# A decoder layer on one core: the context blocks loaded a pair ahead into other rooms, and the last quarter of w_out loaded earlier

## What is computed

```python
# x: (4, 1024, 1024)   ctx_1024: (4, 1024, 512)
qkv = layernorm(x) @ w_qkv                      # 16 heads of 64, causal softmax attention
x = x + attention(qkv) @ w_out
query = ctx_1024 @ Wq.T + bq                    # (4, 1024, 128)
key   = ctx_1024 @ Wk.T + bk
attn  = softmax(query @ key.T)                  # 1024 x 1024
x = x + layernorm(x) @ attn.T
x = x + gated_experts(layernorm(x))             # 8 experts, rank 8, argmax gate
```

## Time and profile before

| what | value |
|---|---|
| median of 3 runs | 2772.9 us (2771.0 to 2775.31) |
| the profiled execution | 2772.5 us, of which the span is 2770.6 us |
| TensorE matmul busy | 2404.3 us (87%) |
| VectorE busy | 1884.6 us (68%) |
| ScalarE busy | 782.0 us (28%) |
| GpSimd busy | 717.5 us (26%) |
| mean granted TensorE clock | 0.954 of full |
| DMA, mean | 146 GB/s |
| chain that ended last, TensorE's share | 59% |

### The profile page before, as it was taken

One profiled execution on the slowest core, in us unless ns is written; L12 is line 12 of the kernel. 1 busy time (PEld: TensorE's weight loads), 2 busy tenths in 40 slices (PEclk: granted clock), 3 DMA queues, 4 the chain that ended last, 5 costly groups with the idle time before them and its releaser, 6 DMA issues.

```text
span 2770.6 us, 37859 instructions
## 1 busy us (share of the span) xinstructions
PE 2404.3 (87%) x14389; PEld 1186.3 (43%) x14389; DVE 1884.6 (68%) x3421; ACT 782.0 (28%) x1557; POOL 717.5 (26%) x981
## 2 busy tenths in 40 slices
PE   0588888689898999869998999969989999986997
PEld 0233444344454444444444444434444444434544
DVE  4577887646876767755786777764696777764566
ACT  1033333321213333322212333431221333332110
POOL 3122433213402222212421222221330222221220
PEclk9899999899999999979999999989999999998997
DMA  6678787856746776775753777774773677776543
GB/s 177 216 174 182 161 214 179 189 140 145 146 108 126 141 151 135 140 181 129 147 125 100 150 139 143 146 186 109 158 147 106 117 149 146 143 154 159 107 76 91
DMA packets 986009, 403.97 MB, mean 146 GB/s; under 512 B 937116, under 2 KB 946332, under 8 KB 985828
## 3 DMA queue, kind: packets, MB, share of 16 engines
q1 hardware_dynamic: 985828, 401.56, 65.8%
HBM read 133.05 MB, written 33.55 MB: 60 GB/s over the span
## 4 chain that ended last, share of the span: by engine, by line
PE 59%; DVE 19%; DMA 10%; issue 6%; ACT 3%; POOL 2%; SPq 1%; ACTq 0%; POOLq 0%; DVEq 0%
PE ps_p L537 8%; PE ps_p L538 8%; PE ps_p L539 8%; DMA r<-pn 8%; PE ps_s L537 6%; PE ps_s L538 6%; PE ps_s L539 6%; PE ps_s L582 6%; PE ps_o L607 5%; DVE pn L816 4%; DVE peak L853 3%; ACT probs L742 2%; DVE bn L821 2%; DMA qk<-in_x 2%; PE ps_s L587 1%
## 5 line engine op out<-in xcount | busy, mean ns | idle before, releaser
L1080 POOL TENSOR_SCALAR pn<-probs,rden 128x640 f16<-128x640 f32 (+7 forms) x512 | 391.9, 778 | 1332.7 <-DVE rden L865 827.1
L742 ACT ACTIVATE probs<-ps_s,low,back 128x640 f32<-128x640 f32 (+7 forms) x512 | 421.7, 827 | 950.8 <-DVE low L856 840.1
L816 DVE SCALAR_TENSOR_TENSOR pn<-probs,rden,pn 128x640 f16<-128x640 f32 (+7 forms) x512 | 476.3, 962 | 193.1 <-POOL pn L1080 192.8
L537 PE MATMUL ps_p<-r,w 128*128 128x512 f16 x1344 | 515.1, 383 | 3.1 <-DVE qk L816 3.1
L538 PE MATMUL ps_p<-r,w 128*128 128x512 f16 x1344 | 514.2, 383 | 0.0
L539 PE MATMUL ps_p<-r,w 128*128 128x512 f16 x1344 | 513.7, 382 | 0.0
L582 PE MATMUL ps_s<-qk 64*128 64x512 f16 (+3 forms) x2304 | 239.0, 332 | 107.9 <-ACT probs L742 97.9
L853 DVE TENSOR_REDUCE peak<-ps_s 128x2 f32<-128x1280 f32 (+3 forms) x128 | 241.4, 1886 | 92.8 <-PE ps_s L587 90.3
L607 PE MATMUL ps_o<-r,vn 128*64 128x512 f16 (+3 forms) x2304 | 210.9, 339 | 39.3 <-issue 30.0
L539 PEld LDWEIGHTS ps_p<-r,w 128*128 128x128 f16 x1344 | 132.5, 99 | 162.1 <-issue 6.3
L582 PEld LDWEIGHTS ps_s<-qk 64*128 64x128 f16 x2304 | 90.0, 95 | 252.3 <-ACT probs L742 147.4
(11 more groups left out here) (167 smaller groups left out, 3554.0 us busy)
## 6 DMA issues: line engine op xcount, KB each, us to landing
w<-w_pairs SPq DMA_DIRECT2D x72, 512.0 KB, 4.0
qk<-in_x SPq DMA_DIRECT2D x32, 512.0 KB, 4.3
r<-wo_pairs SPq DMA_DIRECT2D x16, 1024.0 KB, 7.3
w_raw<-in_x SPq DMA_DIRECT2D x32, 512.0 KB, 4.6
out<-r SPq DMA_DIRECT2D x32, 512.0 KB, 2.9
r<-in_w_qkv SPq DMA_DIRECT2D x24, 512.0 KB, 5.8
w_raw<-in_w_qkv SPq DMA_DIRECT2D x24, 512.0 KB, 5.1
w_pairs<-w SPq DMA_DIRECT2D x24, 512.0 KB, 5.5
```

The costliest lines, as they stand in the source:

```text
L537: pe.matmul(ps, lh, rh, start=start and k == ks[0], stop=False)
L742: act.activation(probs_part(q, j, w), ps_s[:, j, scores(q)], ACT.Exp, bias=low[:, n % 2, i:i + 1], scale=sc, accum_out=den[:, n % 2, i:i + ...
L816: dve.scalar_tensor_tensor(out=to, in0=bank, scalar=scale, in1=rounded, op0=ALU.mult, op1=ALU.subtract).then_inc(ok, 1)
L1080: pool.tensor_scalar(to, src, scale, 1.0, ALU.mult, ALU.mult).then_inc(ok, 1)
```

## The change

Three things change, in every tail.

`ctx_raw` becomes the two rooms of `w_raw`. JI0 and JI1 stand behind T6 of the pair before, ahead of KI; they wait for the last raw weight (batch 0) or the last output of the batch before. JI2 and JI3 wait until JL0 and JL1 are through. RI0 and RI1, which use the same rooms, now wait for JL2 and JL3, and stand behind T5 and T6. Each room has its own semaphore.

OI3 stands behind T2, where it waits for nothing that is open.

The steps JH, JL, G, QH and QL stand earlier in the strings of ScalarE, VectorE and TensorE: G0 where it was, G1 ahead of M0, G2 ahead of B00, G3 behind S7, and B10 straight behind B01.

```diff
 PE_TAIL = """
-    S2 S3 M1- S4 G0 S5 M0 S6 G1 B00 S7 B01 G2 B10 G3 B11 M1 B20 N0 B21 N1 B30 N2 ...
+    S2 S3 M1- S4 G0 S5 G1 M0 S6 G2 B00 S7 G3 B01 B10 B11 M1 B20 N0 B21 N1 B30 N2 ...
 DVE_TAIL = """
-    X0 L70- L71- CL21 R0 X1 L00 L01 X2 R1 L10 L11 R2 X3 KL L20 L21 OL1- R3 JL0 X4 L30 L31 R4 X5 QL0 JL1 L40 L41
-    R5 OL0 X6 L50 L51 QL1 JL2 R6 X7 L60 L61 R7 RA0 L70 L71 QL2 JL3 RA1 QL3 LB0 OL1 CX0 LL0 LB1 CR0 RA2 CX1 CLO0
+    X0 L70- L71- CL21 R0 X1 L00 L01 X2 R1 L10 L11 R2 X3 KL JL0 R3 OL1- X4 L20 L21 QL0 JL1 R4 L30 L31 X5 L40
+    L41 QL1 JL2 R5 OL0 X6 L50 L51 R6 QL2 JL3 X7 L60 L61 R7 QL3 RA0 L70 L71 RA1 LB0 OL1 CX0 LL0 LB1 CR0 RA2 CX1 CLO0
 ACT_TAIL = """
-    E00 E01 CH21 E10 E11 E20 E21 KH E30 E31 JH0 OH1- E40 E41 QH0 JH1 E50 E51 OH0 E60 E61 QH1 JH2 E70 E71 QH2 JH3
+    E00 E01 CH21 E10 E11 E20 E21 KH JH0 E30 E31 OH1- QH0 JH1 E40 E41 E50 E51 QH1 JH2 OH0 E60 E61 QH2 JH3 E70 E71
 SP_TAIL = """
-    OI0 JI0 OI1 T0 T1 OI2 T2 JI1 T3 T4 JI2 RI0 RI1 OI3 T5 JI3 T6 T7 WD0+ WD1+ WD2+ RI2 RI3 ...
+    OI0 OI1 T0 T1 OI2 T2 OI3 JI2 T3 T4 JI3 T5 RI0 T6 RI1 T7 WD0+ WD1+ WD2+ RI2 RI3 ...
 for pair in range(PAIRS - 2, BATCH * PAIRS, PAIRS):
-    ONCE["SP", pair, "T6"] = "KI"
+    ONCE["SP", pair, "T6"] = "JI0 JI1 KI"
-        ctx_raw = vt16[:, :, :].rearrange("p s d -> p (s d)").bitcast(F32).rearrange("p (c d) -> p c d", c=CC)
+        ctx_raw = w_raw[:, :, :].rearrange("p s (c d) -> p s c d", c=CC)
                     elif kind == "JI":
-                        if i > 0:
-                            sp.wait_ge(j_ok, 4 * b + i)
-                        else:
-                            sp.wait_ge(v_in, 16 * PAIRS * (b + 1))
-                        sp.dma_start(ctx_raw[:, :, :], ctx_t[b, :, :, i * CQ:(i + 1) * CQ]).then_inc(j_in, 16)
+                        if i >= 2:
+                            sp.wait_ge(j_ok, 4 * b + i - 1)
+                        elif b == 0:
+                            sp.wait_ge(w_ok, 3 * PAIRS)
+                        else:
+                            sp.wait_ge(y_ok, TB * b)
+                        sp.dma_start(ctx_raw[:, i % 2, :, :], ctx_t[b, :, :, i * CQ:(i + 1) * CQ]).then_inc(j_in[i % 2], 16)
                     elif kind == "RI":
                         if i >= 2:
                             sp.wait_ge(x1_ok, T - 1)
-                        elif b == 0:
-                            sp.wait_ge(w_ok, 3 * PAIRS)
-                        else:
-                            sp.wait_ge(y_ok, TB * b)
+                        else:
+                            sp.wait_ge(j_ok, 4 * b + 3 + i)
```

More of the change, by code:

```diff
@@ L58 @@
 PE_TAIL = """
-    S2 S3 M1- S4 G0 S5 M0 S6 G1 B00 S7 B01 G2 B10 G3 B11 M1 B20 N0 B21 N1 B30 N2 B31 N3 B40 N4 B41 N5 B50 N6 B51 N7
+    S2 S3 M1- S4 G0 S5 G1 M0 S6 G2 B00 S7 G3 B01 B10 B11 M1 B20 N0 B21 N1 B30 N2 B31 N3 B40 N4 B41 N5 B50 N6 B51 N7
     B60 B61 B70 B71 Z00 Z01 Z10 Z11 Z20 Z21 F0 Z30 Z31 F1 D0 Z40 Z41 F2 D1 U0 Z50 Z51 F3 D2 U1 Z60 Z61 F4 D3 U2
@@ L86 @@
 SP_TAIL = """
-    OI0 JI0 OI1 T0 T1 OI2 T2 JI1 T3 T4 JI2 RI0 RI1 OI3 T5 JI3 T6 T7 WD0+ WD1+ WD2+ RI2 RI3 CT0 LT0 CT1 RI4
+    OI0 OI1 T0 T1 OI2 T2 OI3 JI2 T3 T4 JI3 T5 RI0 T6 RI1 T7 WD0+ WD1+ WD2+ RI2 RI3 CT0 LT0 CT1 RI4
     LT1 RI5 CT2 CT3 RI6 CT4 CT5 RI7 CT6 CT7 AI0+ AI1+ AI2+ AT0+ AT1+ AI3+ LT2 AT2+
@@ L280, in decoder_layer @@
         d_bn, d_mv, d_ve, d_rs, d_sh, d_xn, d_hi, d_lo, t3_in = sems("d_bn d_mv d_ve d_rs d_sh d_xn d_hi d_lo t3_in")
-        k_in, kh_ok, kl_ok, j_in, jh_ok, j_ok, g_mm, qh_ok, ql_ok = sems(
-            "k_in kh_ok kl_ok j_in jh_ok j_ok g_mm qh_ok ql_ok")
+        k_in, kh_ok, kl_ok, jh_ok, j_ok, g_mm, qh_ok, ql_ok = sems(
+            "k_in kh_ok kl_ok jh_ok j_ok g_mm qh_ok ql_ok")
+        j_in = [sem(f"j_in{s}") for s in range(2)]
         n_mm, n_peak, n_low, ce_ok, n_den, n_r, n_hi, n_lo = sems("n_mm n_peak n_low ce_ok n_den n_r n_hi n_lo")
@@ L491, in rest @@
                     elif kind == "JI":
-                        if i > 0:
-                            sp.wait_ge(j_ok, 4 * b + i)
-                        else:
-                            sp.wait_ge(v_in, 16 * PAIRS * (b + 1))
-                        sp.dma_start(ctx_raw[:, :, :], ctx_t[b, :, :, i * CQ:(i + 1) * CQ]).then_inc(j_in, 16)
-                    elif kind == "RI":
                         if i >= 2:
-                            sp.wait_ge(x1_ok, T - 1)
+                            sp.wait_ge(j_ok, 4 * b + i - 1)
                         elif b == 0:
@@ L503, in rest @@
                             sp.wait_ge(y_ok, TB * b)
+                        sp.dma_start(ctx_raw[:, i % 2, :, :], ctx_t[b, :, :, i * CQ:(i + 1) * CQ]).then_inc(j_in[i % 2], 16)
+                    elif kind == "RI":
+                        if i >= 2:
+                            sp.wait_ge(x1_ok, T - 1)
+                        else:
+                            sp.wait_ge(j_ok, 4 * b + 3 + i)
                         sp.dma_start(x_res[:, i % 2, :], x[b, i]).then_inc(xr_in[i % 2], 16)
@@ L763, in rest @@
                     elif kind == "JH":
-                        act.wait_ge(j_in, 16 * (4 * b + i + 1))
+                        act.wait_ge(j_in[i % 2], 16 * (2 * b + i // 2 + 1))
                         if i > 0:
@@ L768, in rest @@
                             act.wait_ge(s_ok, TB * (PAIRS * (b + 1) - 1))
-                        act.activation(ctx_hi[:, :, :], ctx_raw[:, :, :], ACT.Copy).then_inc(jh_ok, 1)
+                        act.activation(ctx_hi[:, :, :], ctx_raw[:, i % 2, :, :], ACT.Copy).then_inc(jh_ok, 1)
                     elif kind == "QH":
@@ L1011, in rest @@
                         dve.wait_ge(jh_ok, 4 * b + i + 1)
-                        dve.tensor_tensor(ctx_lo[:, :, :], ctx_raw[:, :, :], ctx_hi[:, :, :].bitcast(F32),
+                        dve.tensor_tensor(ctx_lo[:, :, :], ctx_raw[:, i % 2, :, :], ctx_hi[:, :, :].bitcast(F32),
                                           ALU.subtract).then_inc(j_ok, 1)
```

## The result

The changed kernel takes 2711.9 us (median of 4 runs, 2706.59 to 2712.79), the kernel before beside it 2772.85 (4 runs, 2771.0 to 2775.31). The ratio is 0.9776, with a 95% interval from 0.9759 to 0.9793: faster by 61 us (57 to 67), where 70 were forecast (2703). The profiled execution took 2711.69 us, with a span of 2709.8.

What follows compares the result with a forecast made beforehand. The prediction took TensorE's waits before B00, G0 and M1, 85.0 us over four tails, as the bound on each tail's first stretch. Four tails of 17.5 us make 70, from 2772.5 to 2702.5, predicted as 2703 us, range 2690 to 2722.

Steps and rivals of the forecast that it cites:

- B00's wait: Before the output projection's first product: 10.51 us in the first tail, ended by OI3's landing; OI3 would now land about 546.
- G0: First context product: no longer waits for JL0, starts about 533.5, takes 3.0 us, through at 536.5 against 547.0.
- The added wait before S5: TensorE idle 3.7 us while ScalarE does a QH and a JH step before the exponentials, which end at 540.2.
- the part on the clock: Half clock after S5's gap costs S5 and G1 3.6 us, hidden if T3 lands at 548.3; lasting longer, 4 us more.
- T3: Transpose M0 waits for: issued 541.9, landed 548.3 behind OI3 and JI2, at most 551.8; M0 waits about 3.8 us.
- M0 and S6: On TensorE ahead of G2: 1.8 and 1.3 us, in a row of 21.0 us to B01's end at 569.3.
- The first rival: Late loads (T3 near 551.8) or lasting half clock take back 3.5 to 4 us per tail: 2719 us; chance 0.16.
- B10's new wait: B10 straight behind B01 waits for RA0, which G2 had covered: 1.5 us with handovers.
- M1: Starts 581.2 to 582.3 in the first tail, against 599.53; 17.5 us per tail taken.
- Only B00's wait goes: Rival: QH and JH steps ahead of the exponentials give back G0's gain; 10.5 us per tail, 2731 us; chance 0.07.
- the wait only changes its name: Rival: OH0 stands behind JH2, which needs JI2, now queued behind OI3; no gain, 2773 us; chance 0.04.
- the case for slower: Late RI0 stops TensorE in B10; slower if it lands past 587, 2785 us at 590; chance 0.03.

Runs made afterwards that it cites:

- combined kernel: Changed kernel with stand-ins, plus OI3 behind T3, G3 between B01 and B10, QL3 behind L71: 2681.3 us, 0.9660 of the kernel before.
- stand-ins: Seven kernels with each DMA transpose replaced by a plain copy of as many bytes in pieces of 256 bytes: 2681.3 to 2760.2 us.
- last kernel: Combined kernel plus exponentials ahead of QH and JH steps on ScalarE, one VectorE step earlier, JI0 and JI1 behind T4: 2683.1 us, 0.9670.
- both controls: Kernel before and changed kernel, each with stand-ins and no other edit: 2760.2 us (0.9940) and 2693.9 us (0.9713).

## Why the prediction was right

The waits that were to go went, and those that were to come came, each at its place. Of the 9 us that are missing from the 70, 5.7 lie between M1- and M1, most of them half clock in M0 and S6, and 3.5 elsewhere. Point by point, in the first tail.

*B00's wait.* It went as forecast, and for the cause named: OI3 landed 6.5 us after its issue at 537.59, at 544.1, 11.2 us before B00 started at 555.30. OI3 alone moved takes this wait away and no other.

*G0.* Forecast straight behind S4, at 533.5, at full clock. It came at 531.85, 533.47 on the clock of before, and ran at a granted clock of 1.00. This did not bring M0 forward, which T3 holds; it made room for G1 ahead of M0.

*The added wait before S5.* Forecast 3.7 us, measured 3.61. The engine was at half clock in S5 behind it (0.50) and back at 1.00 in G1, and T3's landing hid that loss, as the part on the clock had it. In the fourth tail the half clock went on through most of G1, and T3's landing hid that as well.

*T3.* Forecast issued at 541.9 and landed at 548.3. It was issued at 540.42 (542.04) and landed at 547.5 (549.1): the issue was right, the landing 0.8 us late. **This term was mis-sized:** 7.1 us from issue, 6.4 taken. M0 followed G1 after 3.43 us, where 3.8 had been forecast; G1's end was 1.3 us late too (544.20, 545.8 on the clock of before, for 544.5), by the half clock in S5.

*M0 and S6.* Forecast 3.1 us. **This is the larger mis-sized term:** in tails 1, 2 and 4 they took 4.7, 4.7 and 4.6 us, at half clock for the greater part, 1.6, 1.6 and 1.5 more; in tail 3 nothing. The prediction weighed the clock only at the gap before S5, and priced M0 and S6 at full clock although its own sum has 3.8 us of idle time ahead of M0. The first rival, at 0.16, had the half clock of S5 go on through M0, S6 and G2, some 4 us in every tail. That is not what happened: in the first tail the clock was 1.00 through G1 and through the idle time behind it (the row from 544.20), and fell anew 0.7 us into M0. The loss came in three of four tails, and was over before B00. The section of the Trainium skill that the prediction names ("TensorE: Matmul & The Clock Gate", "Why this matters for your kernels") says that idle gaps between bursts of matmuls put the engine back to half clock. The trace agrees for S5's gap of 3.61 us and for M0's of 3.43, 3.91 and 2.99; behind 3.22 us in the third tail the clock stayed at 1.00.

*B10's new wait.* Forecast 1.5 us, measured 1.38, four times. The combined kernel, where G3 covers RA0, is without it.

*M1.* Forecast at 581.2 to 582.3. It started at 582.24, 583.9 on the clock of before, straight behind B11. T7 was issued at 574.13 and landed 6.7 us later, at 580.8, so it was in time, as forecast. Against the 581.2 of the row of matmuls M1 is 2.7 us late: 0.9 of it came with M0's start (549.25 for 548.3), 1.6 with the half clock in M0 and S6. In the third tail, without that loss, M1- itself ran 0.9 us longer than in the first (at half clock for more of it), so that tail is not shorter by as much.

*JI0 and JI1 ahead of KI.* Forecast at no cost, with 3.4 us in a tail as the worst. M1- waited 3.51, 3.20, 3.40 and 3.27 us for T7 of the pair before, against 2.88, 3.44, 2.82 and 2.83: 1.4 us more over four tails. That JI0 and JI1 cause it is not shown. With the stand-ins, loading them ahead of T5, so long before T7, made no difference, and the waits of the four tails together lie side by side: 10.9 and 11.6 us in the two kernels that load neither a pair ahead, 11.7 to 12.7 in the four that load them ahead of T7. The cause stays open.

From M1- to M1 the four tails took 73.81, 75.76, 73.62 and 74.27 us before and 58.14, 58.89, 57.33 and 58.81 after: 15.7, 16.9, 16.3 and 15.5 us less, 64.3 in all, where four times 17.5 had been taken. The first M1- starts 1.6 us earlier than before, and the three stretches from M1 to the next M1- took 578.1, 578.5 and 579.1 us before and 579.8, 581.5 and 579.6 after, 5.1 more, of which 0.8 is M1-'s wait. 64.3 and 1.6 less 5.1 are the 60.8 by which the spans differ. The forecast took the stretches behind M1 as unchanged; what made them longer was not found.

*The other rivals.* "Only B00's wait goes" and "the wait only changes its name" did not come. JI2 landed 7.2 us after its issue, at 545.7; JH2 started at 545.76 straight behind QH1, and G2, which needs that block, only at 552.35. RI0, the case for slower, kept nobody waiting: B10's wait is ended by RA0 after 1.38 us, which is RA0's own length.

## What to carry to other kernels

Follow a wait that the profile puts down to "issue" by hand: list what the waiting instruction needs. The load that landed within a tenth of a us of the start is the suspect, and moving it alone is the test; here one word in SP's string was worth 36 us by itself. A load that has landed early gains little until the step that reads it is also early on its own engine: the rooms without the new order gave 4.7 us of G0's 28. When a load is moved forward past a wait, look at which transpose it now stands ahead of, and let the transpose go first if the load has slack: T3 ahead of OI3, with G3 as cover for RA0, gave 14.7 us with the stand-ins. It was not run with transposes. In the changed kernel M0 waits 13.6 us in all (3.43, 3.91, 3.22, 2.99), B10 5.5, and M0 and S6 lose 4.7 to the clock: 23.8, less the 0.9 that M0 still waits in the combined kernel. So between 14 and 23 us below 2711.9 is an estimate. And a wait removed ahead of another wait is worth only the work that can be moved into it: G0 had waited some 8.3 us in each tail, and M0, held by T3, came no earlier for its going.

## What was not expected of the hardware

The clock that follows a gap on TensorE can't be told from its length alone. Behind 2.99 us before M0 the engine was at half clock, behind 3.22 us in another tail of the same execution at full. In the second tail of the last kernel gaps of 1.81 and 1.57 us, the second's end 2.9 us behind the first's, were followed by 5 us at half clock; in its third tail gaps of 1.68 and 1.57 us left G1 at 1.00, as one of 0.83 and one of 1.55 us had in the kernel before. Nor need the clock fall within the gap: ahead of M0 in the first tail it stood at 1.00 for the whole 3.4 us without work, and the loss was paid in the matmuls behind it.

A plain copy between tiles in pieces of 256 bytes lands about as fast as the transpose of as many bytes: 4.1 us for 512 KB against T3's 4.3. Still both controls are about 17 us faster than the kernels that they stand for, by the ratios (0.9940 against 1, and 0.9713 against 0.9776). In the pair of after M0's waits are part of it: 7.9 us in all in the control, 13.6 in the changed kernel. In the pair of before it is G0's and B00's, 28.0 and 39.9 us in the control against 33.2 and 42.8. The rest was not followed.
